# One rise per group of products: the signals that TensorE gives in a mixture-of-experts stage, from eight for an expert and a dense piece to five

## The reference

```python
cap = max(1, int(CAP_FACTOR * N * K / E))          # 640 rows for each of 32 experts
xe  = xp[buf_tok].reshape(E, cap, DIM)             # the tokens that chose the expert
h   = jax.nn.silu(einsum('ecd,edh->ech', xe, w1)) * einsum('ecd,edh->ech', xe, w3)
out = einsum('ech,ehd->ecd', h, w2) * buf_w.reshape(E, cap, 1)
y   = zeros.at[buf_tok].add(out)
z   = jax.nn.silu(xf @ sw1) * (xf @ sw3) @ sw2     # the shared expert, for every token
return y + z
```

## Time and profile before

| | us |
|---|---|
| median of 3 runs | 905.85 (905.0 to 906.47) |
| span of the profiled execution, first to last instruction | 977.5 |
| TensorE busy in that span | 859.0 |
| VectorE, ScalarE, GpSimd busy | 654.3, 616.8, 673.5 |

### The profile page before, as it was taken

The page is one execution under the profiler, slowest core; times in us unless marked ns, Lnnn a source line. Parts: engine busy times, 40 slices in busy tenths (PEclk is TensorE's granted clock), DMA queues, the critical chain, the costliest instruction groups (busy, mean ns, idle before and its releaser), DMA issues. The chain is left out here.

```text
span 977.5 us, 25690 instructions
## 1 busy us (share of the span) xinstructions
PE 859.0 (88%) x9439; PEld 633.9 (65%) x9439; DVE 654.3 (67%) x2448; ACT 616.8 (63%) x1189; POOL 673.5 (69%) x580
## 2 busy tenths in 40 slices
PE   5789999999999999999999999766688888888654
PEld 2367777777777777777777777654465666666422
DVE  7757788987987987987987986836243434343217
ACT  3668889888888888888898787733132323233305
POOL 7656665699698699699689689346665555556636
PEclk9989999999999999999999999978798989899968
DMA  5787788645444454354354342016333323333147
GB/s 160 182 255 234 231 243 220 177 107 134 97 119 111 101 135 108 89 151 107 73 141 122 72 117 64 21 51 197 119 96 100 96 79 95 95 101 99 39 191 252
DMA packets 104428, 126.62 MB, mean 130 GB/s; under 512 B 22077, under 2 KB 65426, under 8 KB 103408
## 3 DMA queue, kind: packets, MB, share of 16 engines
q1 hardware_dynamic: 95408, 109.25, 40.8%
q0 software_dynamic: 8896, 15.74, 5.2%
HBM read 33.68 MB, written 41.58 MB: 77 GB/s over the span
## 5 line engine op out<-in xcount | busy, mean ns | idle before, releaser
L2289 POOL TENSOR_TENSOR PL<-PF,PH 128x1280 f16<-128x1280 f32 x121 | 317.8, 2626 | 107.2 <-ACT PH L1632 63.7
L1854 DVE CUSTOM_DVE_ANT_0 JUNK<-PS,M 128x256 f16<-128x256 f32 (+3 forms) x512 | 225.2, 485 | 39.5 <-PE PS L1265 35.8
L1626 ACT ACTIVATE PF<-PS 128x512 f32<-128x512 f32 (+1 forms) x384 | 192.8, 520 | 80.3 <-PE PS L1298 75.4
L2332 POOL DMA_INDIRECT y_rows<-BIG,Q x150 | 145.7, 972 | 99.3 <-ACT BIG L1551 57.4
L1632 ACT ACTIVATE PH<-PF 128x1280 f16<-128x1280 f32 x128 | 162.2, 1267 | 0.6
L2322 POOL DMA_INDIRECT xe_rows<-PAY,DEST x128 | 129.3, 1010 | 42.9 <-issue 27.7
L1291 PE MATMUL PS<-Q,K 128*128 128x512 f16 (+3 forms) x512 | 148.6, 300 | 9.2 <-DMA Q<-MROW 4.9
L1315 PE MATMUL PS<-VH,PH 128*128 128x65 f16 x1280 | 141.3, 195 | 13.0 <-DVE Y L1896 8.5
L1317 PE MATMUL PS<-VH,PL 128*128 128x65 f16 x1280 | 141.3, 194 | 1.2 <-issue 1.2
L1315 PEld LDWEIGHTS PS<-VH,PH 128*128 128x128 f16 x1280 | 119.6, 98 | 35.0 <-issue 24.5
L1316 PE MATMUL PS<-VL,PH 128*128 128x64 f16 x1280 | 141.3, 194 | 0.0
(11 more groups left out here) (252 smaller groups left out, 2027.5 us busy)
## 6 DMA issues: line engine op xcount, KB each, us to landing
K<-KH SPq DMA_DIRECT2D x128, 128.0 KB, 2.3
Q<-QH SPq DMA_DIRECT2D x128, 128.0 KB, 2.4
xe_rows<-PAY SPq DMA_DIRECT2D x20, 520.0 KB, 4.2
Q<-xe_rows SPq DMA_DIRECT2D x30, 325.0 KB
K<-KL SPq DMA_DIRECT2D x64, 128.0 KB, 2.3
Q<-QL SPq DMA_DIRECT2D x64, 128.0 KB, 2.3
y_rows<-PAY SPq DMA_DIRECT2D x16, 512.0 KB, 4.9
K<-in_L_ffn_w_dram SPq DMA_DIRECT2D x96, 64.0 KB
```

What stands on the lines that cost most here:

```text
L1626: e.activation(PF[:, n % PBUF, c0:c0 + width], PS[:, k, 0:width], ACT.Exp).then_inc(s["c_exp"], 1)
L1854: e.tensor_tensor_reduce(JUNK[:, n_ttr % 2, 0:width], PS[:, base + ab, c0:c0 + width], M0[:, 512 - width:512], 1.0, -3e38, ALU.add, ALU.ma ...
L2289: e.tensor_tensor(PL[:, n % PBUF, :], PF[:, n % PBUF, :], PH[:, n % PBUF, :], ALU.subtract).then_inc(s["c_lp"], 1)
L2332: e.indirect_dma_start(out=y4[:, :], out_offset=bass.IndirectOffsetOnAxis(ap=XE[:, x_ % 6, k, 128:129].bitcast(I32), axis=0), in_=OUT[:, x ...
```

## The change

The rises in the middle of a group go. `s_hid` is raised once an expert, behind the last of the four matmuls of `hidden`; `s_o` once, behind the fifth tile of `product`; `s_dup` once a piece, behind the second product of `dense_up`. The waits on them are counted anew. No instruction is added, taken away or moved on any engine: TensorE has 7395 rows of instructions in its listing before and after, ScalarE 933, VectorE 2138, GpSimd 327 and SyncE 321.

```diff
-    def rows_done(x_, k=4):
-        if x_ < 0:
-            return 0
-        return 2 * x_ + (1 if k < 3 else 2)
+    def rows_done(x_):
+        return max(x_ + 1, 0)
...
                 for hf in range(2):
                     i = e.matmul(PS[:, bank + hf, 0:320], EW[:, x_ % 4, m, :], XET[:, x_ % 2, hf * 320:(hf + 1) * 320],
                                  start=True, stop=True)
-                i.then_inc(s_hid, 1)
+            i.then_inc(s_hid, 1)
...
                 for k in tiles:
                     i = e.matmul(out_of(k), HS[:, x_ % 2, k * 128:(k + 1) * 128], EW[:, x_ % 4, 2, :],
                                  start=True, stop=True)
-                i.then_inc(s_o, 1)
+            i.then_inc(s_o, 1)
...
             for m, bank in ((0, one), (1, two)):
-                e.matmul(PS[:, bank, :], weights(d, m), X1TA[:, t], start=True, stop=True).then_inc(s_dup, 1)
+                u = e.matmul(PS[:, bank, :], weights(d, m), X1TA[:, t], start=True, stop=True)
+            u.then_inc(s_dup, 1)
...
         def silu(x_):
-            w.wait_ge(s_hid, 2 * x_ + 1)
+            w.wait_ge(s_hid, x_ + 1)
...
             for k in range(5):
-                w.wait_ge(s_o, rows_done(y_, k))
+                w.wait_ge(s_o, rows_done(y_))
...
         def dense_silu(i):
-            w.wait_ge(s_dup, 2 * i + 1)
+            w.wait_ge(s_dup, i + 1)
...
         def turned(x_):
             w.wait_ge(s_turn, x_ + 1)
-            w.wait_ge(s_hid, 2 * (x_ - 1))
+            w.wait_ge(s_hid, x_ - 1)
...
         def times(x_):
-            w.wait_ge(s_hid, 2 * x_ + 2)
+            w.wait_ge(s_hid, x_ + 1)
...
         def dense_times(i):
-            w.wait_ge(s_dup, 2 * i + 2)
+            w.wait_ge(s_dup, i + 1)
```

## The result

The changed kernel took **916.19 us** (median of 4 runs, 914.73 to 918.22) beside 906.16 us for the kernel before (905.0 to 907.42): a ratio of 1.0117, with a 95% interval of 1.0096 to 1.0137. It is slower by about 10.0 us; 9.75 were forecast.

What follows compares the result with a forecast made beforehand. TensorE was taken to bound the kernel, busy 88% of the span. Terms 0 + 8.1 + 0.45 + 1.2 = 9.75 us on 905.85 gave 915.6 us; own range 912 to 918, whole range 906 to 920.

Steps and rivals of the forecast that it cites:

- The price of a turn: Turn with a piece: waits ahead of `turn` and `dense_down` lie side by side, 0.45 us longer, 7.20 for 6.75.
- The turns that count: Prolonged turns 7 to 24 ahead of GpSimd's last wait: 18 x 0.45 = 8.1 us, plus 0.45 in expert 23.
- The head: Loop's first experts: 0.74 us later at expert 2, 0.45 for small waits in experts 3 to 5; 1.2 us.
- A rise for nothing: TensorE's matmuls: a rise costs them nothing, so removing 81 gives 0.0 us; bound 0.8 us.
- GpSimd as a cover: Experts 3 to 23: GpSimd needs 127.4 us, TensorE 130.8, so GpSimd hides 0 of the longer turns.
- I take the late signals to belong to the profiled execution: Late TensorE signals among the experts assumed absent from timed runs, which were forecast from on-time turns of 6.75 us.
- Eight late turns at 11.29: Profiled expert turns: eight at 11.29 us less 6.75 explain 36 us of the span's excess over the timed median.
- the gap of 71.7 us: Whole kernel: profiled span 977.5 us against timed median 905.85; 71.7 us taken as not in the timed executions.
- the second rival: Expert turns: late signals are real in timed runs and fewer rises bring fewer; 13.6 us back, 902 us; chance 0.12.

Runs made afterwards that it cites:

- E2: Kernel before with only `s_o` raised once an expert, behind the fifth tile of `product`: 916.44 us, ratio 1.0110.
- E3: Kernel before with only `s_dup` raised once a piece: 910.69 us, ratio 1.0047.
- E1: Kernel before with only `s_hid` raised once an expert: 907.07 us, ratio 1.0008.
- E12: Kernel before plus 333 further TensorE rises that nobody waits for, on a slow chip: 975.37 us beside 973.83, ratio 1.0007.
- E4: Kernel before with `product`'s tiles split 2 and 3 between banks 6 and 7, in place of 3 and 2: 903.63 us, ratio 0.9980.
- E7: The changed kernel again, beside the kernel before on a slow chip: 968.17 us beside 975.49, ratio 0.9940.
- E9: Changed kernel with the 81 rises put back on a semaphore nobody waits for, slow chip: 963.35 us beside 974.46, ratio 0.9913.
- E10: Kernel before with only `s_hid` raised once an expert, on a slow chip: 979.64 us beside 974.46, ratio 1.0070.
- E11: Kernel before with `product`'s tiles split 2 and 3, on a slow chip: 974.11 us beside 974.46, ratio 1.0044.
- E5: Kernel before, unchanged, with a new profile, on a slow chip: 975.6 us beside 978.53 for its twin, ratio 0.9956; span 972.7.

## Why the prediction was right, and where it was not

- **The price of a turn** was right: 0.45 forecast, 7.20 for 6.75 measured, with `turn` waiting 0.37 for `dense_times`, `dense_down` for the third copy, and the two side by side. E2 and E3 show each alone (7.20 and 7.02; 7.20 and some 7.02 forecast).
- **The turns that count** were right: 18 x 0.45 and 0.45 make 8.55. From `hidden` of expert 2 to the last scatter's end it is 196.8 us after and 188.2 in E1, whose head takes as long (681.81 to 870.04): 8.6.
- **The head** was 1.2 and came to 1.2 to 1.4. Its parts were sized less well: the way from expert 2 to expert 3 grew by 0.6 to 0.8 (5.93 for 5.30 and 5.13) where 0.74 was forecast, and the next three by 0.6 where 0.45 was; a wait of 0.34 ahead of a `hidden` is for silu and not, as forecast, for HS in its second half.
- **A rise for nothing**: right for the matmuls (`hidden` at 2.32 with one, two and four rises). The Trainium skill, "TensorE: Matmul & The Clock Gate", section "The cost: per-tile semaphore tail", has 26.3 ns for each. By that the twelve further rises of a turn in E12 would be some 0.3 us, an estimate; its on-time turn is 6.75 as before.
- **GpSimd as a cover** hid nothing, as forecast. That it stands right behind was confirmed by E4, where 6 us of TensorE's time gave 2 to 3.
- **The step that failed** is "I take the late signals to belong to the profiled execution". They were there in every profile on chips where the timed runs are slow as well, and in none on the others. "Eight late turns at 11.29" was a misreading too: of the 19 turns with a piece six take over 11 us and four 8.1 to 8.4, and 17 of the missing us lie ahead of the experts, where nothing was looked for. The number came out because the timed runs were made on a chip without late signals, as the gap of 71.7 us had let suspect; to that extent it was luck. On a chip with them the same change gives 5.9 us back (E7), which is the sign of the second rival, though not its reason, the number of rises (E9).
- **Why the change is faster on such chips** was not shown. One reading is that TensorE's waits of 0.37 us at each `turn` shorten the delays: E7 and E9 have them and are faster, E10 and E11 haven't and aren't. No run put in such a wait without delaying a signal, and E2 and E3 were not run on such a chip, so the later signals of `product` and of the pieces are as good a reading. What holds the signals up stays open as well.

## What to carry to other kernels

A signal in the middle of a group is worth what stands in the queue that waits for it: of three that were taken away one cost nothing in a turn with a piece, for its result is needed a turn later (and 1.2 to 1.4 us at the loop's head, where it is needed at once). One lay on a wait that TensorE stood in already, `dense_down` for the third copy, and one on a wait with 0.2 us to spare (`dense_times` was done at 810.70 and `turn` began at 810.92). Price such signals together, not one by one, where they hold up the same engine. And where a profile's span is far from the timed median, first find out whether both come from the same kind of chip: here the change costs 10 us on one kind and gives 6 back on the other.

## What was not expected of the hardware

The same kernel took 906 us on one chip and 974 to 979 on three others. Its two profiles, of 977.5 and 972.7 us, are both of the slower kind. In them the engines behind TensorE start late, by up to 5 us, at every second to third turn, while TensorE's next matmuls still start on time: in E5 `hidden` follows at 767.71, but VectorE takes up the turned tiles only at 769.73, 3.1 us behind the end of `turn` (765.94 + 0.71). That it is the rises that are late is read from this and from waits without a record, not seen directly. Waits of 0.4 us on TensorE go with shorter delays in most turns: 7.98 us for the long turn in place of 10.1 to 11.3.
